# A two-part change to a fused Metaformer kernel: where GpSimd's last payload begins, and 155 expert tiles in place of 156

## The reference

```
x = x + spectral_conv(ln_c(x))             # spherical harmonic transform, mixing of coefficients, inverse
t = tokens(x); t = t + opcode_ffn(ln_t(t)) # nibble arithmetic with one-hot vectors
x = x + spiking_attention(ln_c(x))         # q, k, v and output through leaky integrate-and-fire over 8 time steps
t = tokens(x); t = t + moe(ln_t(t))        # 8 experts, the 2 largest logits, softmax over the two
```

```
logits = x @ Wg + bg
topk_vals, topk_idx = top_k(logits, 2);  topk_w = softmax(topk_vals)
a, g = split(x @ W1[e] + b1[e]);         out_e = (silu(a) * g) @ W2[e] + b2[e]
out = sum over the two chosen experts of topk_w * out_e
```

## Time and profile before

| | us |
|---|---|
| median of three timed runs | 1301.36 |
| the three runs | 1296.43, 1301.36, 1301.63 |
| the profiled execution | 1295.22 |
| its span, first to last instruction | 1293.4 |
| granted TensorE clock, mean of the span | 0.853 |

### The profile page before, as it was taken

One profiled execution on the slowest core, in us unless ns is written; L12 is line 12 of the kernel. 1 busy time (PEld: TensorE's weight loads), 2 busy tenths in 40 slices (PEclk: granted clock), 3 DMA queues, 4 the chain that ended last, 5 costly groups with the idle time before them and its releaser, 6 DMA issues. The chain is left out here.

```text
span 1293.4 us, 23831 instructions
## 1 busy us (share of the span) xinstructions
PE 993.2 (77%) x6645; PEld 837.2 (65%) x6646; DVE 859.4 (66%) x2743; ACT 654.1 (51%) x1400; POOL 564.4 (44%) x731
## 2 busy tenths in 40 slices
PE   9847746876677675867666453099999999999997
PEld 7837644654456464746555342088888888888886
DVE  7707633756579898888984765066766766667665
ACT  3427732454868877687755431044444444444443
POOL 3310000121132575656665667535555555555554
PEclk9978977976878978778787655599999999999999
DMA  9997966940010010000000001111111111111110
GB/s 264 227 248 156 240 171 157 271 103 20 20 50 20 20 47 19 30 16 20 25 12 30 22 19 35 60 33 35 42 46 50 48 50 42 46 48 47 49 37 2
DMA packets 111924, 93.12 MB, mean 72 GB/s; under 512 B 8012, under 2 KB 100556, under 8 KB 111081
## 3 DMA queue, kind: packets, MB, share of 16 engines
q1 hardware_dynamic: 83753, 62.28, 20.5%
q0 software_dynamic: 9088, 17.33, 4.1%
q10 hardware_dynamic: 19008, 12.59, 3.8%
HBM read 55.61 MB, written 38.39 MB: 73 GB/s over the span
## 5 line engine op out<-in xcount | busy, mean ns | idle before, releaser
L1721 POOL DMA_INDIRECT out_dram<-res,index x156 | 155.8, 999 | 217.8 <-DVE res L1787 189.8
L1830 ACT ACTIVATE sil<-ps_h 128x512 f32<-128x512 f32 x156 | 93.1, 597 | 254.8 <-PE ps_h L1882 254.8
L1752 DVE TENSOR_TENSOR act_rows<-ps_h,sil 128x512 f32<-128x512 f32 x156 | 108.0, 692 | 133.4 <-ACT sil L1830 133.4
L1901 PE MATMUL ps_y<-r_raw,aT 128*128 x1248 | 164.8, 275 | 0.0
L1901 PEld LDWEIGHTS ps_y<-r_raw,aT 128*128 128x128 f32 x1248 | 151.6, 192 | 0.1
L160 POOL DMA_INDIRECT slots<-x_sb,r_pos x128 | 129.3, 1010 | 47.7 <-issue 36.0
L1880 PE MATMUL ps_h<-r_raw,uTh 128*128 x312 | 137.6, 441 | 1.6 <-DVE uTl L1746 1.6
L1881 PE MATMUL ps_h<-r_raw,uTh 128*128 x312 | 124.7, 400 | 0.0
L1882 PE MATMUL ps_h<-r_raw,uTl 128*128 x312 | 123.0, 394 | 0.0
L1092 PE MATMUL ps_q<-wqkv,zT 128*128 128x256 f32 x256 | 114.1, 537 | 0.0
L1204 POOL TENSOR_TENSOR x_sb<-x_sb,sy 128x256 f32<-128x256 f32 x64 | 43.8, 684 | 137.1 <-ACT sy L1340 136.9
(11 more groups left out here) (242 smaller groups left out, 2468.7 us busy)
## 6 DMA issues: line engine op xcount, KB each, us to landing
slots<-zero SPq DMA_DIRECT2D x4, 2652.0 KB, 23.2
pay<-slots SPq DMA_DIRECT2D x39, 272.0 KB, 2.8
coefc<-coefficients ACTq DMA_DIRECT2D x16, 256.0 KB, 6.2
mixed<-mo ACTq DMA_DIRECT2D x16, 256.0 KB, 9.1
gin<-mixed SPq DMA_DIRECT2D x16, 256.0 KB, 14.7
r_raw<-in_L_ffn_W SPq DMA_DIRECT2D x8, 508.0 KB
out_dram<-res,index POOLq DMA_INDIRECT x156, 2.2
pana<-in_legendre_analysis SPq DMA_DIRECT2D x1, 2048.0 KB, 12.8
```

Of the source, the lines that this page charges most:

```text
L1721: nc.gpsimd.indirect_dma_start(out_rows, bass.IndirectOffsetOnAxis(at, 0), res[:, m % RES, :], None, bounds_check=TOKENS - 1, oob_is_err=F ...
L1752: nc.vector.tensor_tensor(act_rows[:, k], ps_h[:, k, :, DFF:], sil[:, k], ALU.mult).then_inc(s_act, 1)
L1830: nc.scalar.activation(sil[:, k], ps_h[:, k, :, 0:DFF], ACT.Silu).then_inc(s_sil, 1)
L1901: ins = nc.tensor.matmul(dst, aT[:, k, (2 * e + h) * P:(2 * e + h + 1) * P], raw[:, 4 + h, col], start=(h == 0), stop=(h == 1))
```

## The change

There are two parts.

The first splits `pay` in two. `pay_power` holds the offsets, the difference and order flags, the sum and the power (three links of the chain), and `pay_shares` the rest (two links and the two payload columns). Everywhere but in one place they are called one behind the other, as before. At the end of the stage POOL's queue becomes: gap and `pay_power` of block 6, deviation of block 7, `pay_shares` of block 6, scatters.

The second lets the expert stage work off 155 tiles. The loop over turns stays; the last turn has 11 steps in place of 12 on each of the four engines, and the drain behind it is written for tile 154 as the last one. The buffer, its clearing and the loads of four tiles stay at 156.

```diff
+USED_TILES = NTILES + PAIRS - 1
         def pay(pool, v):
+            pay_power(pool, v)
+            pay_shares(pool, v)
+
+        def pay_power(pool, v):
             chain = Chain(pool, s_share, v * SHARE_LINKS)
...
             chain.link(nc.gpsimd.tensor_tensor(share[:, 0, :], total[:, :], inverse[:, :], ALU.pow))
+            assert chain.n == POWER_LINKS
+
+        def pay_shares(pool, v):
+
+            chain = Chain(pool, s_share, v * SHARE_LINKS + POWER_LINKS)
             chain.link(nc.gpsimd.tensor_tensor(share[:, 1, :], power[:, :], share[:, 0, :], ALU.mult))
...
                 add_output(pool, NP2 - 1, LAST)
+                gap_of(pool, NP2 - 2)
+                pay_power(pool, NP2 - 2)
                 route_deviation(pool, NP2 - 1)
-                gap_of(pool, NP2 - 2)
-                pay(pool, NP2 - 2)
+                pay_shares(pool, NP2 - 2)
                 scatter(pool, NP2 - 2, 0, NT)
...
+    SPARE = SLOT_TILES - USED_TILES
...
                 def turn(i, head=False, last=False):
-                    for m in range(STEPS):
+                    for m in range(STEPS - SPARE if last else STEPS):
...
-                for m in range(3):
-                    scatter(TURNS, m - 3)
+                for m in range(USED_TILES - 3, USED_TILES):
+                    scatter(*divmod(m, STEPS))
...
-                turn_gated(n - 1, 1)
-                expert_out(n - 2, 0, at_out[4:6])
-                expert_out(n - 1, 1, at_out[6:8])
+                turn_gated(n - 1, (n - 1) % 2)
+                for m in (n - 2, n - 1):
+                    q = m % G
+                    expert_out(m, m % 2, at_out[2 * q:2 * q + 2])
```

More of the change, by code:

```diff
@@ L1209, in gap_of @@
             nc.gpsimd.tensor_tensor(gap[:, :], top[:, 1], top[:, 0], ALU.subtract).then_inc(s_gap, 1)
-        SHARE_LINKS = 5
+        SHARE_LINKS, POWER_LINKS = 5, 3
         def pay(pool, v):
+            pay_power(pool, v)
+            pay_shares(pool, v)
+        def pay_power(pool, v):
             chain = Chain(pool, s_share, v * SHARE_LINKS)
@@ L1229, in pay @@
                 .then_inc(s_paid, 1)
-            assert chain.n == SHARE_LINKS
+            assert chain.n == SHARE_LINKS - POWER_LINKS
         def deviation(pool, n):
@@ L1696, in _ @@
                 for k in range(RES):
-                    sp.wait_ge(s_out[k], SLOT_TILES // RES * 16)
+                    sp.wait_ge(s_out[k], (USED_TILES - k + RES - 1) // RES * 16)
             @block.gpsimd
@@ L1812, in _ @@
                 turn(TURNS - 1, last=True)
-                for m in range(2):
-                    first_part(TURNS, m - 2)
-                    result(TURNS, m - 2)
+                for m in range(USED_TILES - 2, USED_TILES):
+                    first_part(*divmod(m, STEPS))
+                    result(*divmod(m, STEPS))
             @block.scalar
@@ L1851, in _ @@
                 turn(TURNS - 1, last=True)
-                copied(SLOT_TILES - 1, 1)
+                copied(USED_TILES - 1, (USED_TILES - 1) % 2)
             @block.tensor
@@ L1932, in _ @@
                 turn(TURNS - 1, last=True)
-                n = SLOT_TILES
+                n = USED_TILES
                 at_out = [pe.snap(r, min_val=0, max_val=(E - 1) * C) for r in behind]
-                turn_gated(n - 1, 1)
-                expert_out(n - 2, 0, at_out[4:6])
-                expert_out(n - 1, 1, at_out[6:8])
+                turn_gated(n - 1, (n - 1) % 2)
+                for m in (n - 2, n - 1):
+                    q = m % G
+                    expert_out(m, m % 2, at_out[2 * q:2 * q + 2])
 _CONSTANTS = spectral_tables()
```

## The result

| | before | changed |
|---|---|---|
| median, 15 runs each, us | 1299.52 | 1289.82 |
| lowest and highest, us | 1290.70, 1301.63 | 1283.88, 1296.43 |
| ratio, 95% interval | | 0.9942, 0.9922 to 0.9961 |
| profiled execution, us | 1295.22 | 1290.99 |
| its span, us | 1293.4 | 1289.1 |

The changed kernel is faster by 0.58%, 7.5 us by the ratio, which is also the difference of the two means; the medians lie 9.7 us apart, and the executions of either kernel spread over more than 10 us. The forecast was 4.7 us, a time of 1294.2 us with a range of 1287.5 to 1300; the measured median lies in it. The spans of the two profiled executions differ by 4.3 us.

The account below looks back on a forecast made before the run. PE was taken to bound the expert stage, POOL the stretch from block 7's deviation to the last scatter. Tile 2.7 plus move 2.0 made 4.7 us, from 1298.9 to 1294.2 us, range 1287.5 to 1300.

Parts of the forecast that it names:

- The start of the move: POOL, end of routing: block 6's gap and power run before block 7's deviation, which starts 0.5 us later.
- The placement takes over: DVE's placement becomes last to arrive, so block 6's scatters begin at 772.6 in place of 777.78 us: 5.2 us earlier.
- Held-up scatters: Block 6's scatters on POOL: 2.3 more held up beside DVE's weight operations, 0.9 us each; 2.1 us lost.
- Rival A: Block 6's scatters aren't held up by DVE's weight operations: gain 6.8 us, time 1292.1, chance 0.20.
- The payload of block 7: On POOL it starts at 796.7 us, beside DVE's placement of block 7; 1.1 us lost.
- The sum of the move: Reordering POOL's queue starts the expert stage's first load earlier: 5.2 - 2.1 - 1.1 = 2.0 us.
- Rival B: The reordering on POOL brings nothing, only the dropped tile gains: 2.4 to 2.7 us, time 1296.3, chance 0.19.
- rival C: Block 7's deviation on POOL waits for a late exponential from ACT: slower, time 1302.7 at 9 us delay, chance 0.04.
- The 3.14 us of idle time: POOL's idle time between block 7's first two scatters stays, but could go or come twice, 3.1 us either way.
- The tile: Expert stage, bound by PE: dropping one of 156 tiles gains 2.7 us, bounds 2.4 and 3.0.
- The size: Whole kernel: 4.7 us gain, own range 3.4 to 6.0; chance 0.33 of faster by over 0.5%, 0.64 of the same.

Follow-up runs that it names:

- The whole payload ahead: Changed kernel with block 6's whole payload ahead of block 7's deviation; traced once, no ratio: first load 72.88 us after POOL's last attention output starts, against 71.54.
- The early: Changed kernel with DVE's eight and ACT's four weight operations moved into the last attention steps; ratio to the kernel before 0.9949, again 0.9927.
- the late order: Changed kernel with the twelve weight operations behind the last placement and last exponential; traced once, no ratio: first load 69.65 us after POOL's last attention output starts.
- one scatter less ahead: Changed kernel with the last of block 6's 16 scatters behind block 7's payload; ratio to the kernel before 0.9957.
- the move alone: Kernel before with only the new order on POOL, still 156 tiles; ratio 0.9981 to the kernel before.
- second timing: The changed kernel, unchanged, timed again against the kernel before; ratio 0.9963 (0.9937 to 0.9990).

## Why the prediction was right, step by step

**The start of the move.** Gap 0.63 us behind T0, power 2.58, deviation at 5.60 us; forecast 0.63, 2.59 and 5.60. The deviation is 0.5 us later in relation to T0, as said. Nothing was slower beside DVE's statistics.

**The placement takes over.** First scatter of block 6 at 14.07 us from T0, forecast 14.05, with the releaser that the forecast had asked to see. The whole payload ahead shows the dependence by a dose: 1.3 us of delay to the deviation, 1.2 us at the first scatter, 1.3 us at the load. The win at this point is 5.1 us, more than the 4.42 us of idle time, as the slow steps of the payload no longer run beside the weight operations.

**Held-up scatters.** Forecast 2.1 us lost, bounds 0 and 3. Block 6's scatters take 23.73 us from the first one to the next gap and took 22.03: 1.7 us. The early and the late order show the cause. Rival A, which needed short scatters beside L1041, is out: there the first two take 2.05 and 1.81 us. The Trainium skill, page "SBUF — State Buffer", section "Who interferes with whom", infers that such an operation doesn't hold up the generation of descriptors; the scatters of this kernel were held up. A scatter also reads its row numbers from r_pos, a tile in SBUF, and no run here tells which of the two steps was held up. The same section says that a DVE operation with two inputs in SBUF holds up GpSimd operations that read SBUF, and the three flag operations below agree (1.93 us beside such operations, 0.70 us without).

**The payload of block 7.** Forecast 1.1 us lost, bounds 0 and 1.4; it was 1.6. From its gap to its first scatter it took 805.48 - 796.85 = 8.63 us, before 806.82 - 799.81 = 7.01. This term was mis-sized, and beyond its bound: I had read it from block 6, where the flags took 1.12 us, but here they met three 448-column operations in a row and took 1.93 us. These are the flags of block 6 and of block 7 in the kernel before, and then DVE's three operations beside the flags in the changed kernel (798.20 to 800.13):

```profile
767.55 1.12 POOL L1220 TENSOR_SCALAR order<-rise 128x16 f32<-128x16 f32 x3
800.77 0.70 POOL L1220 TENSOR_SCALAR order<-rise 128x16 f32<-128x16 f32 x3
...
798.08 0.62 DVE L1025 TENSOR_TENSOR place<-place,start 128x448 f32<-128x448 f32 x1
798.74 0.63 DVE L1026 TENSOR_TENSOR place<-place 128x448 f32<-128x448 f32 x1
799.39 0.63 DVE L1027 TENSOR_TENSOR place<-place,chosen 128x448 f32<-128x448 f32 x1
```

How POOL's small operations fall against DVE's decides it: with one scatter less ahead, the power and not the flags stood beside these three operations and took 3.13 us in place of 2.94, and the payload gave 1.3 us back. This term and the one before it missed in opposite ways by about the same (0.5 us too low, 0.4 us too high), and that the sum came out close is luck to that extent.

**The sum of the move.** 2.0 us forecast, 1.8 in the trace; the move alone 1.8 as well. Rival B (nothing won) is out, and rival C too: the exponential ran at 759.93 us, right behind the gap, and block 7's placement was in place at 801.3, 4.2 us ahead of its scatters. The 3.14 us of idle time stayed in all traces.

**The tile.** 2.7 us forecast, bounds 2.4 and 3.0. The ten traces with 155 tiles have 458.3 to 458.9 us from the load to the end, the three with 156 have 461.3 to 461.5, which is 2.7 us between the means. From the first scatter of a result to the last it is 1283.99 - 850.60 = 433.4 us, before 1288.23 - 852.13 = 436.1, which is the 2.7 us of a tile too; the 3.0 of the first two traces holds 0.2 us more from the start of the stage, and traces of one number of tiles differ by up to 0.6 us anyway.

**The size.** 4.7 us forecast, 4.8 in the traces, 0.9963 in the second timing, 0.9942 in the first. The chances were 0.33 for faster by over 0.5% and 0.64 for within it: the first timing fell on the less likely side, the second on the likelier. The mechanism doesn't decide between them: executions of one kernel differ by over 10 us, and with 4.7 us of gain the spread decides on which side of 6.5 us a timing falls. The measured median of 1289.82 us is 4.4 us below the forecast 1294.2. The starting point, 1298.9, was 0.6 us below the measured median of the kernel before, and the two medians lie 5.0 us further apart than the 4.7 us of the forecast.

## What to carry to other kernels

When idle time ahead of a step is filled by moving work in front of it, ask first what stands behind that step on the other engines: here the 4.42 us were filled, and DVE's placement behind the deviation became the last to arrive at once. Then lay the moved stretch against what the other engines do at its new time, operation by operation: 3.3 of the 5.1 us won went to two more scatters beside 1024-column DVE operations and to a payload that had been clear of the 448-column ones. Where one engine's long operations hold up another's and have idle time elsewhere, moving those may be worth more than the change that brought the collision; here it was 4.2 us against 1.8.

## What the runs showed that I had not expected

In the traces, the spread from one execution to the next lies ahead of the routing's end. T0 differs by 9.4 us over thirteen traces (754.94 to 764.36), while T0 to load repeats within 0.2 us for one order and load to end within 0.6 us for one number of tiles. Two stretches of a single trace could tell effects of 2 us for which 12 timed executions were not enough.

A scatter directly behind a payload begins after 0.79 us of idle time where it is the first to wait for payload and placement, and after 0.16 us where it waits for nothing new.

The 3.14 us of idle time between block 7's first two scatters is 3.13 to 3.15 us in every trace. It keeps its place by the count of POOL's instructions, not by the time or by the scatter's place behind a payload. No run changed how many instructions, or how many scatters, stand ahead of it, so whether it would move with either is not shown. What POOL does in it the profile doesn't show, and this stays open.
